# Pads of the second scratch one per tile load, the last norm's pieces a tile apart, a GpSimd drain behind the last scatter, and moments in front of the shift

## What is computed

```python
x = _layernorm(x + _L0_attn_ref(x, ...))       # 16 heads; scores of rank 32, softmax, Wo
x = _layernorm(x + _L0_ffn_ref(x, ...))        # 8 experts, hidden 512

gate_probs = jax.nn.softmax(xf @ gate_w.T, axis=-1)
topk_scores, topk_idx = jax.lax.top_k(gate_probs, 2)
h = jax.nn.relu(jnp.einsum('td,ehd->teh', xf, w1) + b1)
expert_out = jnp.einsum('teh,edh->ted', h, w2) + b2
out = jnp.einsum('ted,te->td', expert_out, combine)   # combine: normalised scores of the best two
```

## Time and profile before

| | |
|---|---|
| median of 3 runs | 1176.12 us (1175.79 to 1178.72) |
| the profiled execution | 1176.31 us, its span 1174.6 us |
| busy | PE 89%, DVE 83%, ACT 76%, POOL 48% |
| second block | until 836 us |
| expert tiles | 837 to 1121 us |
| last scatter to the first sum of the final norm | 1124 to 1130 us |
| final norm and its stores | 1130 to 1169 us |
| last barrier | 1174.6 us |

### The profile page before, as it was taken

One profiled execution on the slowest core, in us unless ns is written; L12 is line 12 of the kernel. 1 busy time (PEld: TensorE's weight loads), 2 busy tenths in 40 slices (PEclk: granted clock), 3 DMA queues, 4 the chain that ended last, 5 costly groups with the idle time before them and its releaser, 6 DMA issues. The chain is left out here.

```text
span 1174.6 us, 24055 instructions
## 1 busy us (share of the span) xinstructions
PE 1045.0 (89%) x7683; PEld 507.6 (43%) x7683; DVE 975.5 (83%) x2024; ACT 896.2 (76%) x1141; POOL 565.2 (48%) x844
## 2 busy tenths in 40 slices
PE   3578989999999999999999989887899989999965
PEld 1112223222222222222322222222599989999932
DVE  4788898999989989899899998984479878888844
ACT  1057878788788787887878878778689988999826
POOL 1224417346264372653725627223267776666644
PEclk9999999999999999999999999999799999999988
DMA  3633232241322423324224232201122232222264
GB/s 87 242 101 90 65 100 75 83 127 54 107 75 80 134 56 100 96 64 124 75 83 115 66 107 71 73 20 34 34 63 78 81 89 76 71 70 58 58 252 182
DMA packets 98799, 106.16 MB, mean 90 GB/s; under 512 B 22107, under 2 KB 76001, under 8 KB 98560
## 3 DMA queue, kind: packets, MB, share of 16 engines
q1 hardware_dynamic: 88032, 82.88, 24.8%
q0 software_dynamic: 8640, 16.93, 4.6%
q10 hardware_dynamic: 2016, 4.98, 1.1%
HBM read 56.46 MB, written 48.38 MB: 89 GB/s over the span
## 5 line engine op out<-in xcount | busy, mean ns | idle before, releaser
L901 DVE TENSOR_REDUCE row_max<-score_ps 128x2 f32<-128x1024 f32 x512 | 618.1, 1220 | 71.3 <-PE score_ps L792 68.3
L861 ACT ACTIVATE probs<-score_ps 128x1024 f32<-128x1024 f32 x512 | 521.7, 1022 | 136.0 <-PE score_ps L774 124.4
L416 PE MATMUL av_ps<-probs,v_one 128*9 128x512 f32 x2048 | 271.9, 603 | 6.2 <-ACT probs L861 6.1
L513 POOL DMA_INDIRECT routed_a<-rows,slot_i x112 | 110.3, 985 | 310.8 <-DVE slot_i L507 244.7
L792 PE MATMUL score_ps<-k_stack,q_stack 48*128 48x512 bf16 x1024 | 203.0, 394 | 55.7 <-ACT probs L861 27.2
L774 PE MATMUL score_ps<-q_stack,k_stack 51*128 51x512 bf16 x1024 | 201.3, 391 | 26.0 <-DVE row_max L901 20.5
L774 PEld LDWEIGHTS score_ps<-q_stack,k_stack 51*128 51x128 bf16 x1024 | 49.2, 93 | 314.9 <-issue 159.2
L1228 ACT ACTIVATE w_cur<-experts 128x1156 f32 x142 | 165.3, 1166 | 13.2 <-issue 7.8
L1384 POOL DMA_INDIRECT y_d<-y_out,place x142 | 141.0, 993 | 60.7 <-issue 58.1
L1167 PE MATMUL up_ps<-xt_sb,w_cur 128*128 128x128 f32 x1136 | 152.5, 278 | 0.6 <-ACT w_cur L1228 0.6
L1175 PE MATMUL down_ps<-w_cur,hidden_r 128*128 128x128 f32 x1136 | 150.8, 276 | 0.0
(11 more groups left out here) (175 smaller groups left out, 1056.6 us busy)
## 6 DMA issues: line engine op xcount, KB each, us to landing
k_stack<-k_stack_d SPq DMA_DIRECT2D x128, 96.0 KB, 2.5
q_stack<-q_stack_d SPq DMA_DIRECT2D x128, 96.0 KB, 2.5
x_rows_sb<-routed_a SPq DMA_DIRECT2D x119, 65.0 KB, 1.9
q_stack_d<-q_parts SPq DMA_DIRECT2D x32, 192.0 KB, 2.9
k_stack_d<-k_parts SPq DMA_DIRECT2D x30, 192.0 KB, 3.1
experts<-expert_rows SPq DMA_DIRECT2D x1, 4624.0 KB, 15.2
x_t<-x_cols SPq DMA_DIRECT2D x16, 256.0 KB, 3.6
q_stack_d<-q_parts SPq DMA_DIRECT2D x32, 128.0 KB, 3.0
```

The costliest lines, as they stand in the source:

```text
L416: last = nc.tensor.matmul(av_ps[32 * g:32 * g + V_COLS, :], v_one[n.parity][:, kb, HG * hg + g, :], probs[:, (2 * j + g // 2) % P_RING, g ...
L513: nc.gpsimd.indirect_dma_start(routed_a if n.c < B - LATE else routed_b, bass.IndirectOffsetOnAxis(ap=slot_i[n.parity][:, w, t:t + 1], axi ...
L861: nc.scalar.activation(probs[:, s % P_RING, :, :], exp_bank(b, s)[:, :, :], ACT.Exp).then_inc(S["exp_done"], 1)
L901: nc.vector.tensor_reduce(row_max[:, m // (STEPS // 2), :, m % (STEPS // 2)], max_bank(b, s)[:, :, :], AX.X, ALU.max).then_inc(S["red_done ...
```

## The change

- `routed_b`'s eight pads are no longer stored together ahead of the load of tile 64: one is stored ahead of each of the loads 64 to 71.
- `layernorm` is split: `residual_sum` stays at tile 4, `statistics` goes to 5, `moments` from 5 to 6, GpSimd's `deviation` from 6 to 7, the last two choose steps of batch 14 from 6 to 7. `scale_out` goes from 8 to 11 to 10 to 13, and everything of batch 15 behind it two tiles later.
- GpSimd drains behind its last scatter.
- In the final norm bn_aggr of batch b stands ahead of the shift of batch b-1.

```diff
+PADS_AT = 64
-            def layernorm(dve, n):
+            def residual_sum(dve, n):
                 ...
                 nc.vector.tensor_tensor(res[:, :, :].rearrange("p t d -> p (t d)"), misc_ps[:, :],
                                         x_bo[:, :, :].rearrange("p t d -> p (t d)"), ALU.add).then_inc(S["res_ready"], 1)
+
+            def statistics(dve, n):
                 dve.wait_ge(S["res_ready"], n.count(1, 1))
                 for t in range(QT):
                     nc.vector.bn_stats(stats[:, t, :], res[:, t, :]).then_inc(S["stats_ready"], 1)
...
                     for t in range(RING, TILES):
-                        if t == 64:
+                        if PADS_AT <= t < PADS_AT + E:
                             sp.wait_ge(table_b, 1)
-                            store_pads(sp, routed_b, CAP_B, LATE * T)
+                            store_pad(sp, routed_b, CAP_B, LATE * T, t - PADS_AT)
...
tensor:
-                        elif j == 13:
+                        elif j == 15:
                             ...
                             x1_to_rows(pe, n15)
-                        elif j == 15:
+                        elif j == 17:
                             ...
                             gate(pe, n15)
-                        elif j == 24:
+                        elif j == 26:
                             ...
                             rank(pe, n15)
...
scalar:
-                        elif 8 <= j <= 11:
-                            scale_out(act, n15, j - 8)
-                        elif j == 13:
+                        elif 10 <= j <= 13:
+                            scale_out(act, n15, j - 10)
+                        elif j == 15:
                             x1_rows_out(act, n15)
-                        elif j == 15:
+                        elif j == 17:
                             logits_out(act, n15)
-                        elif j == 20:
+                        elif j == 22:
                             second_out(act, n15)
...
vector:
                         elif j == 4:
-                            layernorm(dve, n15)
+                            residual_sum(dve, n15)
                         elif j == 5:
+                            statistics(dve, n15)
+                        elif j == 6:
                             dve.wait_ge(S["stats_ready"], n15.count(QT, QT))
                             moments(dve, n15)
-                        elif j == 6:
+                        elif j == 7:
                             for k in (14, 15):
                                 choose(dve, n14, k)
...
-                        elif 16 <= j <= 23:
-                            for k in (2 * j - 32, 2 * j - 31):
+                        elif 18 <= j <= 25:
+                            for k in (2 * j - 36, 2 * j - 35):
                                 choose(dve, n15, k)
...
-                        elif 28 <= j < 28 + TABLE_STEPS:
-                            tile_table(dve, table_b, j - 28, TILES_A, TILES_B, CAP_B, base_b[0:1, :])
+                        elif 30 <= j < 30 + TABLE_STEPS:
+                            tile_table(dve, table_b, j - 30, TILES_A, TILES_B, CAP_B, base_b[0:1, :])
...
                             nc.vector.bn_stats(f_stats[b % 2][:, t, :], sum_ps[b % 4][:, t, :]).then_inc(F["stats"], 1)
-                        if b:
-                            shift_of(b - 1)
                         dve.wait_ge(F["stats"], (b + 1) * QT)
                         for t in range(QT):
                             nc.vector.bn_aggr(f_mv[b % 2][:, t, :], f_stats[b % 2][:, t, :]).then_inc(F["mv"], 1)
+                        if b:
+                            shift_of(b - 1)
                     shift_of(B - 1)
...
gpsimd:
-                        if j == 6:
+                        if j == 7:
                             deviation(pool, n15)
...
                     scatter_y((TILES - 1) % RING)
+                    nc.gpsimd.drain()
                     for b in range(B):
```

More of the change, by code:

```diff
@@ L648, in store_pads, with store_pad @@
                 for e in range(E):
-                    end = sp.value_load(next_row_i[0:1, e:e + 1], min_val=e * cap, max_val=e * cap + rows)
-                    sp.dma_start(routed[bass.ds(end, P), :], pad_rows[:, :]).then_inc(pads_stored, 16)
+                    store_pad(sp, routed, cap, rows, e)
+            def store_pad(sp, routed, cap, rows, e):
+                end = sp.value_load(next_row_i[0:1, e:e + 1], min_val=e * cap, max_val=e * cap + rows)
+                sp.dma_start(routed[bass.ds(end, P), :], pad_rows[:, :]).then_inc(pads_stored, 16)
             def load_tile(sp, t, used):
@@ L884, in body @@
                             if s == 12 and prev:
-                                layernorm(dve, p1)
+                                residual_sum(dve, p1)
+                                statistics(dve, p1)
                             if b.c == B - 1 and 14 <= s <= 14 + TABLE_STEPS:
@@ L1286, in attention @@
                             route(dve, n14, 4)
-                        elif 16 <= j <= 23:
-                            for k in (2 * j - 32, 2 * j - 31):
+                        elif 18 <= j <= 25:
+                            for k in (2 * j - 36, 2 * j - 35):
                                 choose(dve, n15, k)
-                        elif j == 25:
+                        elif j == 27:
                             for k in (0, 1):
                                 route(dve, n15, k)
-                        elif j == 26:
+                        elif j == 28:
                             for k in (2, 3):
                                 route(dve, n15, k)
-                        elif j == 27:
+                        elif j == 29:
                             route(dve, n15, 4)
-                        elif 28 <= j < 28 + TABLE_STEPS:
-                            tile_table(dve, table_b, j - 28, TILES_A, TILES_B, CAP_B, base_b[0:1, :])
+                        elif 30 <= j < 30 + TABLE_STEPS:
+                            tile_table(dve, table_b, j - 30, TILES_A, TILES_B, CAP_B, base_b[0:1, :])
                     def x_out(i, u):
```

## The result

The changed kernel takes 1161.85 us (median of 4 runs, 1161.6 to 1163.04) against 1177.22 us of the kernel before beside it (4 runs, 1175.79 to 1178.72, the three shown ahead of the prediction and one more): ratio 0.9873, 95% interval 0.9861 to 0.9886. The forecast was 1161.3. The profiled execution after took 1161.60 us with a span of 1159.1, against 1176.31 and 1174.6 before.

The account below looks back on a forecast made before the run. TensorE, 89% busy, was taken to bound the expert loop. Pads 5.2, norm pieces 2.7, and final-norm order with drain 6.9 sum to 14.8 us off 1176.12, giving 1161.3 us; range 1159.8 to 1167.

Parts of the forecast that it names:

- Bound and pads: Expert loop: TensorE bounds it; spreading the pads removes tile 64's stall and the slow clock behind it, -5.2 us.
- the cover of 4.6 us: SyncE's queue, tiles 64 to 71: may fall 4.6 us behind before TensorE waits; 2.5 us of it expected used.
- Pieces: Last batch's norm inside the expert loop: moving its parts later removes waits at tiles 6, 12 and 13, -2.7 us.
- What I feared at tiles 5 to 9: Expert loop: VectorE's slack of about 0.3 us a tile nearly used up, so some tenths may come back.
- Rival 2: Expert loop: moved norm parts only move their waits, 1.2 instead of 2.7 us gained; 1163.7 us, chance 0.06.
- Order: Final norm: bn_aggr ahead of the shift makes TensorE the bound at 1.715 us a batch, 1.87 us gained.
- Bank and ScalarE: Final norm: bank returns with 0.2 us of room, ScalarE needs 1.51 us a batch, so neither should hold TensorE's pace.
- Drain: Program's end: a GpSimd drain behind the last scatter costs 0 and makes the closing drain short, 5.0 us gained.
- Rival 3: Behind the last scatter: added drain is held by the loads of y_in, slower at 1183 us; chance 0.04.
- with indirect DMAs issued since the last drain: GpSimd's block-end drains: their 9.1 to 9.3 us go with such DMAs, and not with their age.
- rival 1: Program's end: the second drain costs as much as the first, 1.9 instead of 6.9 us; 1166.3 us, chance 0.19.
- One sign of being wrong: Expert loop: `up` steps above 1.9 us turning up at other tiles would show the prediction wrong.

Follow-up runs that it names:

- e2: Kernel before with only the pads changed, one ahead of each of the loads 64 to 71: 1170.36 us, ratio 0.9961.
- e5: Changed kernel with two pads ahead of each of the loads 64 to 67 instead of one ahead of 64 to 71: 1161.45 us in one run.
- e3: Kernel before with only the pieces of the last batch's norm in the expert loop moved to later tiles: 1172.88 us, ratio 0.9976.
- e4: Kernel before with only bn_aggr of batch b put ahead of the shift of batch b-1 in the final norm: 1173.75 us, ratio 0.9984.
- e1: Kernel before with only a GpSimd drain added behind its last scatter: 1170.94 us, ratio 0.9957.
- e8: Changed kernel with SyncE loading two tiles instead of eight at the end of the attention block: 1161.63 us, ratio 0.9872.
- e7: Changed kernel with two early tile loads instead of eight and four row scatters earlier in each of the attention block's last two batches: 1155.46 us, ratio 0.9827.
- e10: Same kernel as e7, measured again in five more runs: 1156.5 us, ratio 0.9839 to the kernel before.
- e6: Changed kernel with a third GpSimd drain, inside the expert loop in the step of tile 136: 1167.86 us in one run.
- e9: Changed kernel with four more GpSimd drains, in the steps of tiles 8, 24, 56 and 87: 1162.47 us in one run.
- e11: Kernel of e7 with the final norm's second load of y no longer started beside the first: 1156.46 us, ratio 0.9836 to the kernel before.
- e12: Changed kernel with two early tile loads instead of eight and GpSimd drains ahead of the middle block's four late scatters, last two batches: 1159.12 us, ratio 0.9845.

## Why the prediction was right

- **Bound and pads** held. The queue time was 1.11 us an issue where the rows gave 1.10; the stall and the slow clock behind it went together, 5.19 us of trace. e2 gives 4.6 by ratio (2.8 to 6.2), and e5 bears out the cover of 4.6 us. What was mis-sized is how much of it one pad a load uses: 3.96 us, not 2.5, since one pad took 1 us longer than the others. The stall stayed away with 0.6 us to spare, and not with 2.1 (in e2 the queue fell 3.19 us behind): a second pad that takes 1 us more would have reached TensorE.
- **Pieces** held: 2.63 us in the trace against 2.7. What I feared at tiles 5 to 9 did not come (the step behind tile 6 loses 0.40 us in both kernels); what remains is a wait of 0.16 us at the transposes and their own work. Rival 2 is out by e3.
- **Order** held: 1.86 us against 1.87, at the pace of 1.717 us read from the first batches. Bank and ScalarE kept the few tenths of room; e4 shows it without the rest.
- **Drain** held: cost 0, gain 5.06 against 5.0. It was the term with least behind it, as no large drain of the trace before lacked new indirect DMAs in front of it. e1 and e2 are the pair that shows it: with the drain behind the last scatter the closing one takes 1.12 us, without it 10.13. The section of the Trainium skill weighed in the prediction (VectorE: DVE Perf Modes, "The DRAIN you can't avoid") does not describe GpSimd's drains here: they took from 0.60 to 11.74 us as recorded. It speaks of the DRAINs of preamble and postamble, and those here stand at the ends of the program's own blocks or in its GpSimd code.
- **Rival 3**, the drain held by the loads of `y_in`, did not come: the drain ended 9.06 us behind the last scatter although those loads, issued from 1118.1 on, filled the DMA engines (a share of 1.03 and 1.04 in the windows above).
- **What was not in the sum**: 0.67 us from TensorE's clock at the start of the final norm. The gap between the first two stats lies between 1.71 and 2.97 us over the fourteen profiled executions (2.39 in before, 1.72 in after, 2.43 in e1, 2.85 in e4, 1.71 in e8), and I found no edit that it goes with; but only one kernel was profiled twice (e7 and e10: 2.76 and 2.80), so why it differs stays open. That the total came out within 0.6 us is in part luck. The 0.67 together with the sum's 14.8 makes the span's 15.5; the medians of the runs side by side are 1177.22 - 1161.85 = 15.4 us apart, and the forecast was only 0.5 us low since before's median was itself 1.1 us higher with the fourth run than in the three shown first. The parts, not the total, carry the forecast.
- **One reason was incomplete**: "with indirect DMAs issued since the last drain" is right, but it sounded like a price paid or not paid. It is a price per DMA. With that known, rival 1 would have had no place.
- **One sign of being wrong did turn up**: the step behind tile 1 took 0.88 us over the pace, against 0.21 before. It goes with the longer idle time at the barrier, told with the sum above, and not with an edit: the five kernels that idled 4.92 or 4.93 us there (after, e4, e6, e8, e9) lose 0.54 to 0.88 us at that step, the four that idled 2.14 to 2.18 us (before, e2, e3, e5) 0.15 to 0.21; the granted clock was 0.50 in that step after.

## What to carry to other kernels

A GpSimd drain at a block's end costs GpSimd some 0.05 to 0.1 us for each indirect DMA since its last drain (here up to 158 of them), with the other engines waiting at the barrier: look at which engine's drain ends last there, and if it is GpSimd's, put a drain of its own into a stretch in which GpSimd idles at least that long and nobody waits for it. Read the cover first, as in a busy stretch 6.2 of the 8.6 us of such a drain came back in e6. And where two waits end at one time at a barrier (SyncE's loads, GpSimd's drain), taking away one shows nothing: that was seen for the loads (e8); the drain alone, with the loads left, was not run.

## What was not expected of the hardware

- The drain's time goes by the number of indirect DMAs since the last drain, not by their age: 100 row scatters, issued over some 580 us, took 8.49 us to drain, when the last had been issued 4 us before; eight took 0.96. The Trainium skill (Perfetto Trace Analysis, section "DMA Instruction — SWDGE (GPSIMD)") says that the recorded end of such a DMA is that of writing its descriptors and not of the transfer. The trace agrees (2.3 us from issue to landing at 0.96 to 1.18 us of instruction). The landing can explain the 1.2 us that a short drain right behind a scatter has on top, as the drains of e12, with the last scatter landed, lack it; but not the long ones, which take 9.06 us right behind a scatter and 9.08 us 40 us later. What the drain does per DMA stays open.
- Row scatters cost 0.08 us each, result scatters about 0.045 (up to 0.055, if the long drains have no constant part; both are estimates from the rows above); which of their differences matters (destination, row length) was not tried. Nor was it settled why 55 result scatters took 4.56 us where the other rows would give 3.7.
- A shorter idle time in front of a stretch is worth more than itself: with 0.97 us instead of 4.92 at the barrier, the next eight matmuls took 1.13 us instead of 2.04. All fourteen traces fall in these two groups: 0.97 us of idle time and 1.13 us in e7, e10, e11 and e12, 2.14 to 4.93 us of idle time and 2.04 or 2.05 us in the ten others.
